# Softmax self-attention of a Perceiver block: half of the score groups exponentiated on ScalarE straight from PSUM

## The reference

```
def _L2_attn_ref(x, Wqkv, bqkv, Wo, bo, wq, wk):      # 16 heads of 16 channels
    qkv = x @ Wqkv.T + bqkv
    q, k, v = split into heads
    q, k = _rmsnorm(q, wq), _rmsnorm(k, wk)
    attn = jnp.einsum('bqhd,bkhd->bhqk', q, k)
    attn = jax.nn.softmax(attn, axis=-1)               # over the 64 keys of one sequence
    z = jnp.einsum('bhqk,bkhd->bqhd', attn, v)
    return z.reshape(b, s, d) @ Wo.T + bo              # then x = x + this
```

## Time and profile before

| what | value |
|---|---|
| median of 3 runs | 2992.35 us (2987.5 to 2993.35) |
| the profiled execution's own time | 2971.5 us |
| its span, first to last instruction | 2969.7 us |
| TensorE matmul busy | 2556.6 us, 86% |
| VectorE busy | 1806.7 us, 61% |
| ScalarE busy | 1368.2 us, 46% |
| mean granted TensorE clock | 0.924 of full speed |
| this stage in the span | from 2290.8 to 2403.3 us |

### The profile page before, as it was taken

The page is one execution under the profiler, slowest core; times in us unless marked ns, Lnnn a source line. Parts: engine busy times, 40 slices in busy tenths (PEclk is TensorE's granted clock), DMA queues, the critical chain, the costliest instruction groups (busy, mean ns, idle before and its releaser), DMA issues. The chain is left out here.

```text
span 2969.7 us, 83477 instructions
## 1 busy us (share of the span) xinstructions
PE 2556.6 (86%) x35891; PEld 2119.0 (71%) x35891; DVE 1806.7 (61%) x3362; ACT 1368.2 (46%) x3399; POOL 629.7 (21%) x752
## 2 busy tenths in 40 slices
PE   6999778999958999999987839969987767999888
PEld 4888456677747888888876538967764645898567
DVE  6777675566665444444445655667876766776663
ACT  3887324455522433343421314427863344777441
POOL 3111002121012111111102122423331523222200
PEclk9999899999979999999998559988998788999989
DMA  2110012111031000000000042332320001111100
GB/s 76 38 34 17 15 35 67 50 59 31 3 114 44 2 16 16 16 16 16 2 13 12 2 147 91 125 103 89 95 91 0 3 2 51 50 45 46 44 1 29
DMA packets 118220, 126.66 MB, mean 43 GB/s; under 512 B 10877, under 2 KB 110152, under 8 KB 117864
## 3 DMA queue, kind: packets, MB, share of 16 engines
q1 hardware_dynamic: 114024, 110.93, 11.9%
q0 software_dynamic: 3840, 10.49, 1.1%
HBM read 105.67 MB, written 15.73 MB: 41 GB/s over the span
## 5 line engine op out<-in xcount | busy, mean ns | idle before, releaser
L1000 ACT ACTIVATE s_ca_probs<-s_ca_scores,s_ca_neg_max 128x256 f32<-128x256 f32 x768 | 353.5, 478 | 36.3 <-DVE s_ca_neg_max L1044 24.9
L1044 DVE TENSOR_REDUCE s_ca_neg_max<-s_ca_scores 128x4 f32<-128x1024 f32 x192 | 234.3, 1221 | 75.2 <-PE s_ca_scores L910 44.2
L923 PE MATMUL s_ca_probs_flipped<-identity,s_ca_probs 128*128 128x128 f32 x1536 | 213.8, 283 | 11.5 <-ACT s_ca_probs L1000 10.6
L1989 DVE COPY s_mx_w_mixed<-s_mx_ps 128x512 f32<-128x512 f32 x256 | 163.7, 685 | 96.5 <-PE s_mx_ps L1836 83.0
L1375 DVE RECIPROCAL s_cc_inv_sums<-s_cc_sums 128x512 f32<-128x512 f32 x32 | 107.4, 3357 | 182.4 <-PE s_cc_out L1275 182.4
L923 PEld LDWEIGHTS s_ca_probs_flipped<-identity,s_ca_probs 128*128 128x128 f32 x1536 | 167.9, 143 | 53.5 <-ACT s_ca_probs L1000 23.3
L1944 ACT COPY s_mx_w_mixed<-s_mx_ps 128x512 f32<-128x512 f32 x256 | 137.3, 589 | 119.1 <-PE s_mx_ps L1823 94.9
L1195 POOL TENSOR_TENSOR s_cc_probs_of_both<-s_cc_probsT 128x1024 f32<-128x1024 f32 x32 | 76.9, 2403 | 520.0 <-DVE s_cc_probsT L1366 520.0
L836 POOL TENSOR_TENSOR s_ca_inv_spread<-s_ca_inv_sums,h_ca_own_half 128x128 f32<-128x128 f32 x192 | 72.6, 399 | 445.3 <-DVE s_ca_inv_sums L1066 445.3
L1007 ACT COPY s_ca_probsT<-s_ca_probs_flipped 128x512 f32<-128x512 f32 x192 | 115.3, 600 | 99.3 <-PE s_ca_probs_flipped L923 99.3
L1000 ACT ACTIVATION_READ_ACCUMULATOR s_ca_probs<-s_ca_scores,s_ca_neg_max 128x1 f32 x768 | 160.3, 209 | 0.0
(11 more groups left out here) (487 smaller groups left out, 7250.3 us busy)
## 6 DMA issues: line engine op xcount, KB each, us to landing
h_ca_ctxT<-in_ctxT SPq DMA_DIRECT2D x96, 256.0 KB, 3.4
h_mx_w_by_input<-in_L_ffn_eW1T SPq DMA_DIRECT2D x16, 512.0 KB, 5.3
h_mx_w_by_hidden<-in_L_ffn_eW2T SPq DMA_DIRECT2D x8, 1024.0 KB, 6.3
h_re_win<-in_L_ffn_W_in SPq DMA_DIRECT2D x8, 1024.0 KB, 6.1
h_ca_ctx<-in_ctx SPq DMA_DIRECT2D x32, 256.0 KB, 2.7
x_normed_transposed<-in_ctx SPq DMA_DIRECT2D x7, 1024.0 KB, 5.4
h_re_wout<-in_L_ffn_W_out SPq DMA_DIRECT2D x8, 512.0 KB, 3.8
choice_results<-s_rt_zeros SPq DMA_DIRECT2D x4, 1024.0 KB, 10.5
```

The costliest lines, as they stand in the source:

```text
L923: last = nc.tensor.transpose(psT[u % len(psT)][:, 2 * a + c, :], PR[b % 2][:, 4 * n + 2 * h + a, c * P:(c + 1) * P], ident[:, :])
L1000: last = nc.scalar.activation(PR[b % 2][:, p, :], psS[:, p // 2, (p % 2) * NKEY:(p % 2 + 1) * NKEY], ACT.Exp, bias=nmax[b % 2][:, p:p + 1] ...
L1044: nc.vector.tensor_reduce(nmax[b % 2][:, 4 * n:4 * n + 4], psS[:, 2 * n:2 * n + 2, :].rearrange("p r (g k) -> p r g k", g=GR), AX_X, ALU.m ...
L1989: last = nc.vector.tensor_copy(part(int(name[1]), r), bank(j, r))
```

## The change

VectorE still takes the maximum of all 16 groups, now stored negated and in two buffers (`nmax`). It moves only groups 0 to 7 (banks 0 and 1) into `SC`, which is half as large. ScalarE waits for the maxima, then exponentiates groups 8 to 15 directly from banks 2 and 3, with one activation for each group: the negated maximum is the activation's bias, and its accumulated output writes the group's sum into `total`, which now has two buffers. The last of the eight signals a new semaphore, `s_ea`. Then ScalarE waits for the moved half and exponentiates it in one instruction as before. `scores(i)` now waits for both the moved half and the direct exponentials of tile i-1. VectorE sums groups 0 to 7 only; the reciprocal waits for `s_ea` too. Nothing is moved to another place in any engine's list.

```
--- before.py
+++ after.py
@@ -2580,11 +2580,12 @@
         WO, BO, H8, s_w = held.WO, held.BO, held.H8, held.s_w
         PAR = sb("sm_head_parity", [P, 2])
         QB = [sb("sm_q_spread", [P, KC, 2, 2, SEQ]) for _ in range(2)]
-        most = sb("sm_max", [P, 16])
-        SC = sb("sm_scores", [P, 16, SEQ])
+        HALF = 8
+        nmax = [sb("sm_neg_max", [P, 16]) for _ in range(2)]
+        SC = sb("sm_scores", [P, HALF, SEQ])
         EX = [sb("sm_exponentials", [P, 16, SEQ]) for _ in range(2)]
         PR = [sb("sm_probs", [P, 16, SEQ]) for _ in range(2)]
-        total = sb("sm_sums", [P, 16])
+        total = [sb("sm_sums", [P, 16]) for _ in range(2)]
         rinv = [sb("sm_inv_sums", [P, 16]) for _ in range(2)]
         PT = [sb("sm_probsT", [P, 8, P]) for _ in range(2)]
         AT = [sb("sm_attendedT", [P, KC, P]) for _ in range(2)]
@@ -2596,6 +2597,7 @@
                                       sem("scores_ready"))
         s_mx, s_mv, s_e, s_sum, s_ri, s_p = (sem("max_ready"), sem("scores_moved"), sem("exponentials_ready"), sem("sums_ready"),
                                              sem("inv_sums_ready"), sem("probs_ready"))
+        s_ea = sem("direct_exponentials_ready")
         s_t, s_ta, s_td, s_o, s_at, s_y, s_x = (sem("probs_flipped"), sem("first_probsT_ready"), sem("last_probsT_ready"),
                                                 sem("attended"), sem("attendedT_ready"), sem("out_projected"), sem("x_updated"))
 
@@ -2637,6 +2639,7 @@
                     pe.wait_ge(s_q, i + 1)
                     if i:
                         pe.wait_ge(s_mv, i)
+                        pe.wait_ge(s_ea, i)
                     for g in range(KC):
                         for b in range(2):
                             at = i * P + b * SEQ
@@ -2696,10 +2699,16 @@
             @block.scalar
             def _(act):
                 def exponentiate(i):
-                    act.wait_ge(s_mv, i + 1)
+                    act.wait_ge(s_mx, i + 1)
                     if i >= 2:
                         act.wait_ge(s_p, i - 1)
-                    nc.scalar.activation(EX[i % 2][:, :, :].rearrange("p a k -> p (a k)"), SC[:, :, :].rearrange("p a k -> p (a k)"),
+                        act.wait_ge(s_ri, i - 1)
+                    for a in range(HALF, 16):
+                        last = nc.scalar.activation(EX[i % 2][:, a, :], psS[:, a // 4, (a % 4) * SEQ:(a % 4 + 1) * SEQ], ACT.Exp,
+                                                    bias=nmax[i % 2][:, a:a + 1], accum_out=total[i % 2][:, a:a + 1])
+                    last.then_inc(s_ea, 1)
+                    act.wait_ge(s_mv, i + 1)
+                    nc.scalar.activation(EX[i % 2][:, 0:HALF, :].rearrange("p a k -> p (a k)"), SC[:, :, :].rearrange("p a k -> p (a k)"),
                                          ACT.Exp).then_inc(s_e, 1)
 
                 def turned(i):
@@ -2727,21 +2736,24 @@
 
                     dve.wait_ge(s_s, i + 1)
                     four = psS[:, :, 0:4 * SEQ].rearrange("p r (a k) -> p r a k", k=SEQ)
-                    nc.vector.tensor_reduce(most[:, :], four, AX_X, ALU.max).then_inc(s_mx, 1)
+                    if i >= 2:
+                        dve.wait_ge(s_ea, i - 1)
+                    nc.vector.tensor_reduce(nmax[i % 2][:, :], four, AX_X, ALU.max, negate=True).then_inc(s_mx, 1)
                     dve.wait_ge(s_mx, i + 1)
                     if i:
                         dve.wait_ge(s_e, i)
-                    nc.vector.tensor_tensor(SC[:, :, :].rearrange("p (r a) k -> p r a k", r=NR), four,
-                                            most[:, :].rearrange("p (r a) -> p r a", r=NR).unsqueeze(3).broadcast_to([P, NR, 4, SEQ]),
-                                            ALU.subtract).then_inc(s_mv, 1)
+                    nc.vector.tensor_tensor(SC[:, :, :].rearrange("p (r a) k -> p r a k", r=2), four[:, 0:2],
+                                            nmax[i % 2][:, 0:HALF].rearrange("p (r a) -> p r a", r=2).unsqueeze(3).broadcast_to([P, 2, 4, SEQ]),
+                                            ALU.add).then_inc(s_mv, 1)
 
                 def add_up(i):
                     dve.wait_ge(s_e, i + 1)
-                    nc.vector.tensor_reduce(total[:, :], EX[i % 2][:, :, :], AX_X, ALU.add).then_inc(s_sum, 1)
+                    nc.vector.tensor_reduce(total[i % 2][:, 0:HALF], EX[i % 2][:, 0:HALF, :], AX_X, ALU.add).then_inc(s_sum, 1)
                     dve.wait_ge(s_sum, i + 1)
+                    dve.wait_ge(s_ea, i + 1)
                     if i >= 2:
                         dve.wait_ge(s_p, i - 1)
-                    nc.vector.reciprocal(rinv[i % 2][:, :], total[:, :]).then_inc(s_ri, 1)
+                    nc.vector.reciprocal(rinv[i % 2][:, :], total[i % 2][:, :]).then_inc(s_ri, 1)
 
                 def turned(i):
                     dve.wait_ge(s_t, 2 * i + 2)
```

## The result

In 12 runs of each kernel the median went from 2991.58 to 3001.35 us, 9.8 us more. The ratio, estimated from all the runs, is 1.0039, 95% interval [1.0022, 1.0056]: about 12 us slower (7 to 17), twice the 6 us that the prediction took as the least that can be told from no change. Its likeliest case, no change, did not come.

The account below looks back on a forecast made before the run. Two 5.48 us loops bound full-clock periods, TensorE's own work nearly fills half-clock ones; 13 periods at +0.15 and +0.22 us gave 2.2, plus 0.3 at the end: 2992.35 + 2.5 = 2995 us, "no change", range 2986 to 3014.

Parts of the forecast that it names:

- (1): Sign on ScalarE: READ_ACCUMULATOR and ACTIVATE rows on the new line, 0.29 us from pair to pair.
- (2): Sign on TensorE: scores wait for ScalarE's direct exponentials, where they waited for nothing, and `attend` is not on the path.
- (5): Sign at the stage's start: `scores(2)` comes at the same place after it.
- (3): Sign on VectorE: idle about 1 us a tile in front of the sum, which becomes its largest wait.
- (4): Sign: period 5.6 us at full clock, 7.85 at half; maxima of tiles 2 and 15 about 82.4 us apart.
- The pair: ScalarE's direct exponential over 64 columns with its accumulator read: 0.29 us, ends 0.11 and 0.45; eight are 2.32.
- Rival C: Dearer pairs of activation and accumulator read on ScalarE: slower, 3003 us at 0.37 a pair, 3011 at 0.45; chance 0.20.
- The loop: Scores, output, half of the flips, ScalarE's copy, eight pairs, scores: 5.63 us, +0.15 a period at full clock, +0.22 at half.
- VectorE: Its work falls 1.08 us a tile, but its loop, waiting for ScalarE, stays 5.4 to 5.6, just hidden under 5.63.
- The start: First two tiles finish about 1 us later, covered by GpSimd's work and `scores(2)` waiting for its queries: nothing.
- The clock: TensorE's clock over the 13 periods: mix kept at 0.68 full and 0.32 half in the sum.
- rival A: TensorE's clock stays at 1.2 GHz through the loop: 13 periods of 7.85 us, +22, 3014 to 3015 us; chance 0.13.

## Why the prediction was right and where it was wrong

The time, 3001 us, lies in its range, 2986 to 3014, but not for the reason of its sum. The sum had +2.5 us, 2.2 of it the longer loop; that loop is there and costs 3.5, and another 10.1 came through the clock, which the sum held fixed. The range was wide enough because a rival put its edge there. Of its signs, (1), (2) and (5) came in the main, (3) with twice the wait, (4) not: periods of 5.76 and 7.99 for 5.6 and 7.85, and 93.8 us for 82.4. The stage's clock fell by 0.08, just under the 0.1 that it had named as showing it wrong. That the time still fell in the range is in part luck.

- *The pair, right.* 0.29 us as taken from rows 7 and 8. By the formula of the Trainium skill ("ScalarE: Activation LUTs", "What ACT_TABLE_LOAD costs") it would be 0.34, an estimate. The formula gives 333 ns for such an activation, and the 128 of them lasted 327 ns in the median, so its duration agrees. The step to the read, 0.20, is 0.04 shorter than its overlap of 93 ns makes it. Rival C is out.
- *The loop, right in kind, too short.* +0.15 and +0.22 were forecast, +0.28 and +0.36 measured. In the full-clock period above the starts of the new loop up to the first direct exponential (output, flips, copy, exponential) are within 0.01 us of the forecast. The last read is 0.25 long for 0.21, and the scores follow 0.14 after it for 0.05. No row stood behind the 0.05; the rows before show 0.10 between the end of VectorE's copy and `attend`. In 13 periods: 3.5 us (shown at equal clocks) for 2.2.
- *VectorE, right in kind.* The sum and the subtraction take 686 and 692 ns, and the relief is eaten: VectorE waits 33.1 us, 2.1 a tile (1.73 in the full-clock period), in front of its sum; I had said about 1. There its maximum starts 0.46 after the scores' end, not 0.07, since the sum, the reciprocal and the statistics come before it; it ends at 2340.34, and ScalarE, busy with its copy, uses it only at 2340.70, so VectorE does not set the period.
- *The start, right:* `scores(2)` begins 14.83 us after the stage's first instruction on VectorE in both kernels. *The end*, +0.3 forecast: from the last maximum to the last statistics 15.00 before and 14.97 after, nothing.
- *The clock, wrong: the step that failed.* The sum weighted the periods with 32% at half clock, as before the change. It was as much as 65% would be: (93.79 / 13 - 5.76) / (7.99 - 5.76). That is 10.1 of the 13.6 us; rival A's price, +22, was for a loop wholly at half clock. Rival A named the mechanism and the stage that hinted at it, and I gave it 0.13, since "the longest pause hardly grows". The longest pause even fell, from 1.65 to 1.49; but a second of 0.37 came, and together they grew to 1.86. In the kernel before the clock was already at an edge, as one idle reduction of 0.33 us shows. The Trainium skill, "TensorE: Matmul & The Clock Gate", section "HAM oscillation — how this bites in real kernels", has waits between bursts of matmuls bring the clock down. These runs agree; there the waits are for DMA, here for VectorE and ScalarE, and none in the full-clock periods is over 1.97 us.

## What to carry to other kernels

Where rows show a stage that swings between the two clocks, a few tenths of waiting on TensorE more or less can be worth several times their length (here 0.33 us a period cost 10.1 us in 13): price every added wait at both clocks and with the share between them moved. Before work is moved to an idle engine, look what stands in front of it in that engine's list and who waits behind it; here the same split lost 0.39% in one order, and won 0.3% with a copy moved to another engine and VectorE's list in another order. A cheap test tells the clock's part from the loop's: put idle matmuls in the pause.

## What the runs showed that I had not expected

More matmuls made the loop faster: two idle ones a tile took 18.3 us off the 13 periods of the changed kernel and 8.2 off those of the kernel before. The loop's time repeated to 0.01 us in the kernel before and to 0.75 in the changed one, in executions whose routed expert layer differed by 11 us, so a stage can be read far more finely than a kernel's time. The variant without the sums on ScalarE warns against taking one profile for all executions.
